# Attention and mixture of experts on one core: the routing of the first batch moved ahead of a wait, its scatters two units earlier, and the last batch's denominators and heads loaded in parts

## What is computed

```python
def _L0_attn_ref(x, ...):            # x is layernorm(input)
    c_kv = x @ W_DKV
    k, v, q = c_kv @ W_UK, c_kv @ W_UV, x @ W_UQ       # 16 heads of 16
    scores = where(causal, einsum('bqhd,bkhd->bhqk', q, k) * scale, -inf)
    ctx = einsum('bhqk,bkhd->bqhd', softmax(scores), v)
    return ctx @ W_O
x = x + _L0_attn_ref(_layernorm(x), ...)
# experts, on xf = layernorm(x)
    logits = xf @ Wr / temp
    topw, topi = top_k(logits, 2);  topw = softmax(topw)
    for e in range(8):
        a, g = split(xf @ W1[e] + b1[e]);  y = a * silu(g) @ W2[e] + b2[e]
        out = out + y * sum(where(topi == e, topw, 0))
x = x + out
```

## Time and profile before

| | us |
|---|---|
| median of 3 runs | 1137.48 (1136.86 to 1139.58) |
| the profiled execution: its own time | 1139.49 |
| its span in the trace | 1137.8 |
| PE busy | 1024.5 (90%) |
| DVE busy | 763.4 (67%) |
| ACT busy | 502.0 (44%) |
| POOL busy | 406.9 (36%) |

### The profile page before, as it was taken

How to read it: one execution, slowest core, us unless ns; L and a number is a source line. 1 busy time by engine, 2 the same in 40 slices (tenths; PEclk the granted TensorE clock), 3 DMA queues, 4 the chain that set the end, 5 groups by cost and what they waited for, 6 DMA issues and landing times.

```text
span 1137.8 us, 19232 instructions
## 1 busy us (share of the span) xinstructions
PE 1024.5 (90%) x5236; PEld 527.9 (46%) x5237; DVE 763.4 (67%) x2270; ACT 502.0 (44%) x1060; POOL 406.9 (36%) x777
## 2 busy tenths in 40 slices
PE   5998999999999999999597532999999999999994
PEld 2443233333333333334355430566666666666663
DVE  3776999999999999997454650555555555555552
ACT  2553277777777777776254431222222221222211
POOL 5566333333333333333234474122222222222222
PEclk9997599999999999999688655999999999999998
DMA  2869756656566544407545984122222222222222
GB/s 90 259 227 272 139 129 131 132 129 133 128 137 125 92 89 88 86 27 177 153 133 149 323 295 133 29 47 44 46 43 45 46 46 46 46 46 43 45 43 27
DMA packets 104058, 125.66 MB, mean 110 GB/s; under 512 B 26480, under 2 KB 82416, under 8 KB 103984
## 3 DMA queue, kind: packets, MB, share of 16 engines
q1 hardware_dynamic: 90688, 107.01, 38.4%
q0 software_dynamic: 13296, 17.77, 9.4%
HBM read 74.47 MB, written 49.89 MB: 109 GB/s over the span
## 4 chain that ended last, share of the span: by engine, by line
PE 80%; DVE 6%; POOL 5%; DMA 4%; issue 3%; ACT 1%; SPq 0%; POOLq 0%; DVEq 0%
PE bank L1756 22%; PE bank L790 12%; PE bank L772 12%; PE bank L811 12%; PE bank L1773 10%; POOL slot_rows L1168 4%; PE bank L1764 3%; DMA c_heads<-ctx_cols 2%; PE bank L1485 2%; DVE a_xn L314 2%; PE a_ckv L363 1%; PE bank L1744 1%; DVE bank L700 1%; PE a_k_ps L379 1%; DVE b_neg_max L703 1%
## 5 line engine op out<-in xcount | busy, mean ns | idle before, releaser
L746 ACT ACTIVATE b_prob<-bank 128x512 f32<-128x512 f32 (+3 forms) x768 | 311.8, 509 | 88.5 <-PE bank L790 87.7
L772 PE MATMUL bank<-b_k_st,b_q_st 96*128 96x512 bf16 (+3 forms) x768 | 255.6, 346 | 5.5 <-DVE b_neg_max L700 1.7
L656 POOL TENSOR_SCALAR_AFFINE_SELECT b_prob<-b_prob 128x128 f32<-128x128 f32 x512 | 146.8, 295 | 316.4 <-ACT b_prob L746 311.7
L1756 PE MATMUL bank<-w_sb,e_rowsT 128*128 x568 | 258.1, 597 | 0.4 <-issue 0.4
L700 DVE CUSTOM_DVE_ANT_0 bank<-bank,b_mask_max 128x256 f32<-128x256 f32 (+3 forms) x512 | 241.3, 507 | 22.9 <-PE bank L772 22.9
L790 PE MATMUL bank<-b_q_st,b_k_st 99*128 99x512 bf16 (+3 forms) x768 | 243.6, 334 | 3.7 <-ACT b_prob L746 1.7
L1649 POOL DMA_INDIRECT out_dram<-e_y,e_token x71 | 110.5, 1556 | 320.6 <-DVE e_y L1703 295.2
L703 DVE TENSOR_REDUCE b_neg_max<-bank 128x1 f32<-128x512 f32 x256 | 175.6, 686 | 13.7 <-PE bank L772 11.1
L1756 PEld LDWEIGHTS bank<-w_sb,e_rowsT 128*128 128x128 f32 x568 | 103.3, 192 | 104.2 <-issue 104.2
L811 PE MATMUL bank<-b_prob,b_v_aug 128*32 128x512 f32 (+3 forms) x1536 | 146.8, 500 | 2.5 <-POOL b_prob L656 2.5
L1773 PE MATMUL bank<-w_sb,e_hiddenT 128*128 x568 | 134.4, 379 | 1.8 <-ACT e_hiddenT L1726 1.8
(11 more groups left out here) (166 smaller groups left out, 900.7 us busy)
## 6 DMA issues: line engine op xcount, KB each, us to landing
w_sb<-in_L_ffn_W SPq DMA_DIRECT2D x12, 1024.0 KB, 5.1
e_rows<-slot_rows SPq DMA_DIRECT2D x72, 129.0 KB, 2.1
ctx_cols<-b_ctx_out SPq DMA_DIRECT2D x16, 512.0 KB
q_parts<-a_part_q SPq DMA_DIRECT2D x8, 768.0 KB, 4.0
k_parts<-a_part_k SPq DMA_DIRECT2D x8, 768.0 KB, 4.8
b_q_st<-q_parts SPq DMA_DIRECT2D x16, 384.0 KB, 4.9
b_k_st<-k_parts SPq DMA_DIRECT2D x16, 384.0 KB, 8.0
a_x<-in_L_attn_x SPq DMA_DIRECT2D x8, 512.0 KB, 5.1
```

The costliest lines, as they stand in the source:

```text
L656: nc.gpsimd.affine_select(out=prob[n % NP][:, 0:P], in_=prob[n % NP][:, 0:P], compare_op=ALU.is_ge, fill=0.0, base=0, pattern=[[1, P]], ch ...
L746: nc.scalar.activation(prob[n % NP][:, 0:width], prob_ps[n % NS][:, 0:width], ACT.Exp, scale=SCALE).then_inc(prob_ok, 1)
L772: nc.tensor.matmul(out[:, 0:width], q_st[g % RING][0:STACK, h, i * P:(i + 1) * P], k_st[g % RING][0:STACK, h, half * HALF:half * HALF + wi ...
L1756: last = nc.tensor.matmul(out_ps[:], rowsT[c % 2][:, d * P:(d + 1) * P], w1_sb[:, bass.ds(expert, 1), d, first:first + FF].rearrange("p e ...
```

## The change

Four things change, and none of the arithmetic.

1. On DVE, `first_normalise()` now stands ahead of `scale_heads(1)` instead of behind it.
2. `SCATTER_AT` was a bound (units from `TOTAL - 4` on) and is now a range of four units that begins at `TOTAL - 6`: the same eight scatters of batch 0 begin two units sooner.
3. The denominators of the last batch are loaded, inverted, stored and read back as scale in two parts. The first 12 heads (three quads) are done ahead of the store of quad 15, in `sync_third`; `store_x2(1)` now comes behind their inverse. The last 4 heads follow in `sync`. DVE inverts the first part behind `scale_heads(2)`, and the second in `residual(2)` after its first addition, not its second.
4. The last batch's heads come in three transfers instead of one, and ahead of the last inverse and scale instead of behind them.

```diff
--- before.py
+++ after.py
@@ -647,8 +647,9 @@
                 v_copy(g + 1)
             if unit == ROOT_AT:
                 route.inverse_root(pool)
-            if unit >= SCATTER_AT:
-                route.first_scatter(pool, (2 * (unit - SCATTER_AT), 2 * (unit - SCATTER_AT) + 1))
+            if unit in SCATTER_AT:
+                n = SCATTER_AT.index(unit)
+                route.first_scatter(pool, (2 * n, 2 * n + 1))
             for n in range(unit * QUAD, (unit + 1) * QUAD):
                 if prob_unit(block_at(n)[0] % UNITS)[4]:
 
@@ -869,7 +870,7 @@
 INVERT_AT = (9 * UNITS + PER_HALF, 13 * UNITS + PER_HALF)
 ROOT_AT = TOTAL - 12
 POWER_AT = TOTAL - 6
-SCATTER_AT = TOTAL - 4
+SCATTER_AT = range(TOTAL - 6, TOTAL - 2)
 
 
 class Route:
@@ -1005,27 +1006,34 @@
         self.turn_ps = [self.banks[5], self.banks[7]]
 
 
-    def load_den(self, sp, b):
+    def load_den(self, sp, b, heads=range(HEADS)):
         if b >= 2:
 
             sp.wait_ge(self.inv_den_ok, b - 1)
-        sp.dma_start(self.den_in[b % 2][:], self.dram["den"][b * HEADS:(b + 1) * HEADS, :].rearrange(
-            "h (t n) -> (h t) n", n=P)).then_inc(self.den_in_ok[b % 2], 16)
-
-    def store_inverse(self, sp, b):
-        sp.wait_ge(self.inv_den_ok, b + 1)
-        sp.dma_start(self.dram["inv"][b * HEADS:(b + 1) * HEADS, :].rearrange("h (t n) -> (h t) n", n=P),
-                     self.inv_den[:]).then_inc(self.inv_den_st, 16)
-
-    def load_scale(self, sp, b):
-
-        sp.wait_ge(self.inv_den_st, 16 * (b + 1))
+        first, last = heads[0], heads[-1] + 1
+        sp.dma_start(self.den_in[b % 2][first * BT:last * BT, :],
+                     self.dram["den"][b * HEADS + first:b * HEADS + last, :].rearrange(
+                         "h (t n) -> (h t) n", n=P)).then_inc(self.den_in_ok[b % 2], 16)
+
+    def store_inverse(self, sp, b, heads=range(HEADS)):
+        sp.wait_ge(self.inv_den_ok, b + 1 + (heads[0] > 0))
+        first, last = heads[0], heads[-1] + 1
+        sp.dma_start(self.dram["inv"][b * HEADS + first:b * HEADS + last, :].rearrange("h (t n) -> (h t) n", n=P),
+                     self.inv_den[first * BT:last * BT, :]).then_inc(self.inv_den_st, 16)
+
+    def load_scale(self, sp, b, heads=range(HEADS)):
+
+        sp.wait_ge(self.inv_den_st, 16 * (b + 1 + (heads[0] > 0)))
         if b:
             sp.wait_ge(self.heads_ok, b * SCALES)
+        per_chunk = P // HD
         for c in range(DC):
-            of = self.dram["inv"][b * HEADS + c * P // HD:b * HEADS + (c + 1) * P // HD, :]
-            sp.dma_start(self.scale[:, c, :], of.unsqueeze(1).to_broadcast([P // HD, HD, SEQ])).then_inc(
-                self.scale_in_ok, 16)
+            these = [h for h in heads if h // per_chunk == c]
+            if these:
+                first, n = these[0], len(these)
+                of = self.dram["inv"][b * HEADS + first:b * HEADS + first + n, :]
+                sp.dma_start(self.scale[first % per_chunk * HD:(first % per_chunk + n) * HD, c, :],
+                             of.unsqueeze(1).to_broadcast([n, HD, SEQ])).then_inc(self.scale_in_ok, 16)
 
     def load_heads(self, sp, b):
         if b:
@@ -1033,6 +1041,13 @@
         context = self.dram["ctx"].rearrange("g (q s) n -> s (g q) n", s=2)[0]
         sp.dma_start(self.heads[:], context[b * D:(b + 1) * D, :].rearrange("(c p) n -> p c n", p=P)).then_inc(
             self.heads_in_ok, 16)
+
+    def load_last_heads(self, sp, c, rows):
+        sp.wait_ge(self.proj_ok, (BATCH - 1) * PAIRS)
+        context = self.dram["ctx"].rearrange("g (q s) n -> s (g q) n", s=2)[0]
+        first = (BATCH - 1) * D + c * P
+        sp.dma_start(self.heads[rows.start:rows.stop, c, :],
+                     context[first + rows.start:first + rows.stop, :]).then_inc(self.heads_in_ok, 16)
 
     def load_x(self, sp, b):
         x = self.sources[0]
@@ -1080,8 +1095,13 @@
     def sync_third(self, sp):
 
         self.load_scale(sp, 2)
+        for p in range(2):
+            sp.wait_ge(self.ctx_st[p], 32 * (NQUAD // 2 - p))
+        self.load_den(sp, 3, range(3 * QUAD))
         self.load_heads(sp, 2)
+        self.store_inverse(sp, 3, range(3 * QUAD))
         self.store_x2(sp, 1)
+        self.load_scale(sp, 3, range(3 * QUAD))
 
     def sync(self, sp):
         _, _, _, _, b_dram, w2 = self.sources
@@ -1090,10 +1110,12 @@
         def load_w2(f):
             sp.dma_start(self.w2_sb[f][:], w2.rearrange("e (f p) n -> f p e n", p=P)[f]).then_inc(self.loaded, 16)
 
-        self.load_den(sp, 3)
-        self.store_inverse(sp, 3)
-        self.load_scale(sp, 3)
-        self.load_heads(sp, 3)
+        self.load_den(sp, 3, range(3 * QUAD, HEADS))
+        self.load_last_heads(sp, 0, range(P))
+        self.load_last_heads(sp, 1, range(P // 2))
+        self.load_last_heads(sp, 1, range(P // 2, P))
+        self.store_inverse(sp, 3, range(3 * QUAD, HEADS))
+        self.load_scale(sp, 3, range(3 * QUAD, HEADS))
         self.load_x(sp, 3)
         self.store_x2(sp, 2)
         for f in range(1, FC):
@@ -1199,13 +1221,15 @@
             self.scatter(pool, b, 1, second_row, self.second_in_slot)
 
 
-    def invert(self, dve, b):
-
-        dve.wait_ge(self.den_in_ok[b % 2], 16 * (b // 2 + 1))
+    def invert(self, dve, b, heads=range(HEADS)):
+
+        first, last = heads[0], heads[-1] + 1
+        dve.wait_ge(self.den_in_ok[b % 2], 16 * (b // 2 + 1 + (first > 0)))
         if b:
 
             dve.wait_ge(self.inv_den_st, 16 * b)
-        self.nc.vector.reciprocal(self.inv_den[:], self.den_in[b % 2][:]).then_inc(self.inv_den_ok, 1)
+        rows = slice(first * BT, last * BT)
+        self.nc.vector.reciprocal(self.inv_den[rows, :], self.den_in[b % 2][rows, :]).then_inc(self.inv_den_ok, 1)
 
     def vector(self, dve):
         nc = self.nc
@@ -1224,8 +1248,9 @@
 
         def scale_heads(b):
 
-            dve.wait_ge(self.heads_in_ok, 16 * (b + 1))
-            dve.wait_ge(self.scale_in_ok, 16 * DC * (b + 1))
+            last = b == BATCH - 1
+            dve.wait_ge(self.heads_in_ok, 16 * (b + 1 + 2 * last))
+            dve.wait_ge(self.scale_in_ok, 16 * (DC * (b + 1) + last))
             for k in range(SCALES):
                 half = slice(k // DC * CHUNK, (k // DC + 1) * CHUNK)
                 nc.vector.tensor_tensor(self.heads[:, k % DC, half], self.heads[:, k % DC, half],
@@ -1242,8 +1267,8 @@
                                         ALU.add).then_inc(self.x2_ok, 1)
                 if t:
                     statistics(b, t - 1)
-                if b == 2 and t == 1:
-                    self.invert(dve, 3)
+                if b == 2 and t == 0:
+                    self.invert(dve, 3, range(3 * QUAD, HEADS))
             last = statistics(b, PAIRS - 1)
             then(last)
 
@@ -1386,13 +1411,14 @@
         self.invert(dve, 2)
         dve.wait_ge(self.small_in, 48)
         then(nc.vector.reciprocal(self.inv_temp[:], self.temp_in[:]))
+        first_normalise()
         scale_heads(1)
-        first_normalise()
         choose(0)
         slots(0)
         residual(1)
         moments(1)
         scale_heads(2)
+        self.invert(dve, 3, range(3 * QUAD))
         for b in range(1, BATCH):
             shift(b)
             if b + 1 < BATCH:
```

## The result

The changed kernel takes 1129.74 us (median of 9 runs, 1128.75 to 1133.62), the kernel before, beside it, 1137.48 (9 runs, 1136.37 to 1140.93). The ratio is 0.9935, with a 95% interval of 0.992 to 0.995: 0.65% faster, 7.4 us by the ratio and 7.7 by the medians. Forecast were 11.5 us and 1126.0.

The account below looks back on a forecast made before the run. The bound was the chain to POOL's 48 scatters, whose start hung on batch 3's heads and earlier waits. Terms 9.5 + 0 + 2.0 = 11.5 us gave median 1126.0, own range 1123.5 to 1129; with overtaking and clock, 1119.5 to 1130.5.

Parts of the forecast that it names:

- First normalise: PE's wait for batch 0's normalised rows: DVE starts them 9.90 us earlier, later choice costs 0.41, gain 9.5 us.
- Scatters: End of attention: PE's 2.48 us wait for POOL's select goes, an upper bound that the later store eats whole.
- Denominators and scale of 12 heads: SP's queue: early scale takes 9.5 us (6.5 to 12), so quad 15 lands at 616 (613 to 619), not 609.1.
- Last heads: From quad 15's landing L, DVE's path and the queue's meet near L + 12.9 = 628.9, not 630.87: gain 2.0 us.
- Sum: Whole kernel: 9.5 + 0 + 2.0 = 11.5 us, profiled execution to 1128.0 and median to 1126.0.
- The store that overtakes the scale: Rival, SP's queue: quad 15's store passes the scale and lands by 608; gain 17 us, 1120.5; chance 0.15.
- The kernel that isn't faster: Rival: DVE's wait for quad 15's denominators eats the 9.5 us, turning at a 24 us store; chance 0.1.
- half of the first part is lost: Rival, project 1: half of the gain returns as waits for ACT or batch 1's heads; 1131; chance 0.1.
- The clock that stays up: Rival, PE after its shortened idle time: a 2.4 GHz clock gives 13 us instead of 9.5, 1122.5; chance 0.15.
- Transposes close behind the inverse root: Sign of being right, on PE: batch 0's first transposes follow the inverse root within 1 us.
- a train without gaps: Sign of being right, on POOL: scatters run without gaps; a gap at batch 2, 2.24 us to spare, means wrong.
- A wait for scale in place of the one for denominators: Sign of being wrong, on DVE: it waits for heads or scale instead of quad 15's denominators.

Follow-up runs that it names:

- before again: The kernel before, unchanged, profiled a second time: 1135.59 us in all for the profiled execution, span 1133.8 us.
- with wide transfers: Changed kernel with heads, scale and W_O in (row, head) order, every scale load 16 rows outermost, in transfers of four heads: 1123.17 us, ratio 0.9859 to the kernel before.
- with both: Last batch's scale loaded as 8 heads early and 8 late, with 16 rows outermost and heads in two transfers: 1123.37 us, ratio 0.9878 to the kernel before.
- the eight-and-eight kernel: Changed kernel with 8 heads' scale loaded early and 8 late instead of 12 and 4: 1124.56 us, ratio 0.9879 to the kernel before.
- without the split: Changed kernel with parts three and four undone, leaving first normalise and scatters: 1124.46 us, ratio 0.9891 to the kernel before.
- the wide layout without the split: Changed kernel, parts three and four undone, scale loads 16 rows outermost: four transfers 1121.02 us (ratio 0.984), two transfers 1120.65 (0.9855).

## Why the prediction was right, and where it was off

The forecast was a gain and the mechanism of its largest term held. The time came out 3.7 us above the predicted one: 0.7 above the forecast's own range of 1123.5 to 1129, and within the 1119.5 to 1130.5 that include two rivals. By its own steps:

*First normalise.* Right. Predicted were an idle time of 2.3 us and 9.5 us of gain; measured 2.48, and 9.70 in the first stretch against the profile before. Against the second profile of before it is 9.0, and 8.3 with the changed kernel's second. The start of PE's row moved by 9.69 us (9.90 predicted). DVE's later choice costs 0.8 (0.41 predicted), and a clock of 0.71 in place of 0.60 gives 0.8 back, which the sum did not have. Alone, this part brought 7.1 at the end: of 9.0 us, 1.5 were given back in the last stretch (22.89 against 21.43) and 0.5 in the second. The transfer of the last heads is not the reason, it took 14.6 us in both profiles. Of the 1.5, 1.0 passes before DVE inverts the denominators (4.05 us behind the issue of their load, 3.02 in before again), while it waits for batch 2's product with `wo`, which took PE 9.96 us in place of 8.83; 0.4 is the inverse on its way. Each of these is one profile, and they may be chance.

*Scatters.* Right in both halves. The term of 2.48 is 2.7 us in the second stretch (25.95 to 23.24), 3.1 at the end where it is alone, and hardly anything of it is left where the split stands ahead of the store: there scatters and split together add 0.4. No kernel has the first normalise and the split without the scatters.

*Denominators and scale of 12 heads.* Right. Predicted was a store of 13 us (613 to 619 on the clock of before); measured 13.27 and 13.25. DVE waits for those denominators, 11.68 us. The middle value between 6.5 and 12 for the scale was a choice that fell right, and the 12 does not follow from its own row: a scale that was issued at 614.7 and crept until 628 took 13.3. That the early scale makes the store late is shown: issued behind the store, it let it land in 4.18. How much of it is its four and eight engines is open. Counted from the scale's issue the store landed after 15.5 us in the changed kernel, after 11.5 with eight heads, after 11.6 with wide transfers and after 11.0 with both; `x2`, the context and the scatters filled the engines beside it in all of them, and no kernel moved those away.

*Last heads.* This is the term that was mis-sized most. From the landing to the multiplication I had 12.9 us, from two paths that meet. DVE's path was as predicted: `choose(1)` ended 3.70 us before the scale had come, 11.8 behind the landing against 12.7. The queue's path was not. The inverse landed 4.78 us after its issue, near what was said (L + 7.3, said L + 7). But the last scale then took 8.12 us, where the prediction had 1.6 plus 4.3, that is 5.9, for "four heads get half of the 123 GB/s". That rate was read from a load that ran alone. In fact `x`, `x2` and the first of three loads of `w2` are issued 0.7 to 1.7 us behind it, and the eight-and-eight kernel shows 8.0 us for twice the size. The landing to the multiplication became 15.49. So the split brought nothing: the changed kernel can't be told from the first normalise alone, and is 5.3 us slower than without the split. Of these 5.3 the stretches show 3.0 and 4.3 in the two profiles; the rest lies outside them and stays open. (The scale's issue, ahead of every edit, alone lies anywhere from 540.35 to 543.17.) That the company of the other loads is the cause for the 2.2 us was only argued: no kernel moved them away. The wide transfer, with the same loads behind it, took 4.4 us at most, so the few engines have their part in it.

*Sum.* Counted from the scale's issue, batch 3's heads are multiplied 78.41 us later, where it was 90.08: 11.7 us sooner, just the 11.5 predicted. This agreement is half luck. The second stretch of that profile of before was 2.5 us longer than in the second profile (28.47 against 25.95), and this hid the 2.6 us that the last term lacked. The step that failed is therefore also "and the median to 1126.0": I moved the profile's slowness to the median as an offset of 2.0 and kept the gain, but the profile was slow in the very stretches that the change touches. Against the second profile of before the gain is 8.1 us, or 6.9 with the second of the changed kernel; the medians say 7.7.

*Rivals.* The store that overtakes the scale is refuted (13.27 us). The kernel that isn't faster too: the store stayed far below the 24 us of its turning point. That half of the first part is lost is refuted at its place. The clock that stays up did not come true: over the same work, from the transposes to the count, it was granted 0.71 in place of 0.60, worth the 0.8 us above, and 0.75 in before again, which idled just as long as before. The 13 us of that rival were not reached: 9.7 at most.

*Signs.* Transposes close behind the inverse root, no wait for POOL's select, a store of 12 us or more, DVE waiting for the denominators, and a train without gaps all came as said. But DVE also waited 3.70 us for the scale. A wait for scale in place of the one for denominators was named as a sign of being wrong; it came beside it, and it is where the last term failed.

A version beats both kernels: the wide layout without the split, 1121.02 us with four transfers and 1120.65 with two, which can't be told apart; some 17 us faster than before.

## What to carry to other kernels

A transfer that is moved forward in a queue is priced by what queues behind it: here 0.79 MB of scale in front of it made a store of 16 KB take 13 us that the last part of the kernel hung on, and 4 us with the scale behind it. A transfer that repeats few rows is made wide by ordering the dimensions, and cutting it into smaller pieces with fewer heads outermost doesn't make it faster. Wide transfers pay where engines are free, not where all of them are busy already. A clock can be compared only over the same work, not over the same microseconds. And take several profiles before a sum is made against one of them: the same kernel's stretches differed by up to 2.5 us.

## What the runs showed of the hardware that I had not expected

- A load that repeats four heads' rows (256 KB) and one of eight (512 KB) took the same time, 8.12 and 8.01 us; with 16 rows outermost the load of eight took 4.5 us at most (610.17 to 614.70, when DVE was free).
- Behind such loads, with others in the queue, small transfers are slow: 16 KB took 12.64 us as a write and 10.81 as a read, against 3.08 and 1.64 without one. A wide load in front did not cure it (8.45 and 10.38 us to the next load's issue): all engines were busy (shares of 1.02).
- PE's granted clock is a mix of its two levels of 1.2 and 2.4 GHz, and the mix over the same work varies between kernels whose order is the same there. From batch 0's first transposes to its count it was 0.51 to 0.79 in four profiles after 12 us without work (20.5 to 15.5 us), and 0.56 to 0.71 in ten after 2.5 us (19.4 to 17.4 us). The same kernel gave 0.60 and 0.75. Once it stayed low with PE busy throughout (the scatters alone):

```profile
560.00:575.00 15.00, 15.00 (x72) 11.10 (x71) 4.35 (x9) 4.37 (x11) 2.85 (x10) 0.50 0.48 146
```
